# The second expert product of a mixture-of-experts block in three rounded parts from the 13th tile on

## The reference

```python
assign = jnp.argmax(x @ centroids.T, axis=1)          # one expert per row
for e in range(8):
    h = _layernorm(xs, ln_g[e], ln_b[e])
    h = jax.nn.relu(h @ w1[e].T + b1[e])              # 256 -> 1024 channels
    ye = xs + h @ w2[e].T + b2[e]                     # 1024 -> 256 channels
    y = y + jnp.where((es == e)[:, None], ye, 0.0)
out_sorted = alpha * y + (1.0 - alpha) * xs
```

## Time and profile before

| | us |
|---|---|
| median of three executions | 635.12 |
| the profiled execution | 630.98 |
| its span, first to last instruction | 629.2 |
| PE busy in the span | 587.4 (93%) |
| DVE busy | 342.7 (54%) |
| ACT busy | 292.6 (46%) |
| `up`, line 1183: PE busy | 147.5 |
| `down`, line 1199: PE busy | 141.8 |

### The profile page before, as it was taken

How to read it: one execution, slowest core, us unless ns; L and a number is a source line. 1 busy time by engine, 2 the same in 40 slices (tenths; PEclk the granted TensorE clock), 3 DMA queues, 4 the chain that set the end, 5 groups by cost and what they waited for, 6 DMA issues and landing times.

```text
span 629.2 us, 12344 instructions
## 1 busy us (share of the span) xinstructions
PE 587.4 (93%) x3638; PEld 499.5 (79%) x3639; DVE 342.7 (54%) x909; ACT 292.6 (46%) x727; POOL 254.5 (40%) x390
## 2 busy tenths in 40 slices
PE   3989999999999999997889998999999999999991
PEld 2557787787877778786789998998999999998980
DVE  1495987959697795988634353333222233322230
ACT  4565758677785867765542522222222222222320
POOL 7706163545646354554333353333333333333321
PEclk9998999999999999996989999999999999999996
DMA  8920111211211020111695575555555545555200
GB/s 311 408 71 1 34 35 34 101 35 69 67 66 37 1 102 1 68 34 67 218 347 166 185 228 208 185 185 193 183 205 217 196 179 182 190 215 190 94 5 0
DMA packets 25186, 83.59 MB, mean 133 GB/s; under 512 B 3821, under 2 KB 13423, under 8 KB 18992
## 3 DMA queue, kind: packets, MB, share of 16 engines
q1 hardware_dynamic: 16896, 59.57, 27.0%
q0 software_dynamic: 7552, 22.89, 10.0%
q10 hardware_dynamic: 688, 0.52, 0.3%
HBM read 70.35 MB, written 13.53 MB: 133 GB/s over the span
## 4 chain that ended last, share of the span: by engine, by line
PE 82%; DVE 6%; issue 3%; POOL 2%; DMA 2%; ACT 1%; DVEq 0%; POOLq 0%; ACTq 0%
PE bank_a L1183 20%; PE bank_l L1199 20%; PE bank_a L958 10%; PE bank_l L946 7%; PE bank_c L1062 4%; PE bank_a L987 4%; PE bank_b L1039 2%; PE bank_a L1003 2%; PE bank_a L996 2%; PE bank_b L1038 2%; DMA arena<-rows_by_expert,take_idx 2%; PE bank_c L1079 2%; PE bank_b L1024 2%; DVE arena L1274 2%; PE bank_b L1171 1%
## 5 line engine op out<-in xcount | busy, mean ns | idle before, releaser
L1183 PEld LDWEIGHTS bank_a<-masks,arena 128*128 128x128 f32 x1248 | 146.7, 194 | 1.8
L1183 PE MATMUL bank_a<-masks,arena 128*128 128x128 f32 x1248 | 147.5, 277 | 0.0
L1571 DVE TENSOR_TENSOR arena<-bank_a,b_col 128x512 f32<-128x512 f32 x78 | 54.0, 692 | 168.8 <-PE bank_a L1183 154.2
L1199 PE MATMUL bank_l<-w_sb,arena 128*128 x624 | 141.8, 380 | 3.0 <-issue 2.0
L1199 PEld LDWEIGHTS bank_l<-w_sb,arena 128*128 128x128 f32 x624 | 115.5, 190 | 18.7 <-issue 4.5
L663 POOL DMA_INDIRECT arena<-rows_by_expert,take_idx x39 | 41.3, 1058 | 156.3 <-DVE k_mix L1585 154.5
L1274 DVE TENSOR_TENSOR arena<-arena 128x256 f32<-128x256 f32 x224 | 93.8, 465 | 7.4 <-PE bank_l L946 7.3
L946 PEld LDWEIGHTS bank_l<-arena,k_mix 128*128 128x128 f32 x448 | 66.1, 198 | 39.6 <-ACT k_mix L712 26.8
L901 ACT ACTIVATE arena<-arena 128x512 f32<-128x512 f32 x78 | 44.9, 622 | 103.5 <-PE bank_l L1199 101.9
L958 PE MATMUL bank_a<-arena 128*128 128x512 f32 x160 | 81.9, 611 | 0.0
L891 ACT ACTIVATE masks<-bank_b,b_col,g_col 128x128 f32<-128x128 f32 x78 | 31.4, 453 | 107.6 <-PE bank_b L1171 107.6
(11 more groups left out here) (151 smaller groups left out, 780.5 us busy)
## 6 DMA issues: line engine op xcount, KB each, us to landing
arena<-w SPq DMA_DIRECT2D x39, 1024.0 KB, 4.8
arena<-x SPq DMA_DIRECT2D x16, 512.0 KB, 3.6
w_sb<-w SPq DMA_DIRECT2D x8, 1024.0 KB, 14.3
arena<-b SPq DMA_DIRECT2D x1, 1024.0 KB, 13.9
arena<-rows_by_expert,take_idx POOLq DMA_INDIRECT x39, 4.7
out<-k_mix,put_of POOLq DMA_INDIRECT x39, 3.7
rows_by_expert<-arena POOLq DMA_INDIRECT x32, 4.3
arena<-wk SPq DMA_DIRECT2D x1, 256.0 KB, 4.2
```

Source lines behind the costliest of these rows:

```text
L1183: m = pe.matmul(bank_a[k // 4][:, k % 4 * P:(k % 4 + 1) * P], w1_now[t.par][:, i * F + k * P:i * F + (k + 1) * P], xl_t[t.par % 2][:, i * ...
L1199: m = pe.matmul(bank_l[p][:, 0:D], h_act[:, k * P:(k + 1) * P], w2_sb[:, bass.ds(e * (FC * D) + k * D, D)], start=(k == 0), stop=(k == FC ...
L1571: dve.tensor_tensor(h_sb[:, n * 512:(n + 1) * 512].rearrange("p (k t) -> p k t", t=P), bank_a[n][:, :].rearrange("p (k t) -> p k t", t=P), ...
```

## The change

From tile 12 on (`in_parts(t)`) the second product is written as a sum of three. ACT no longer writes the relu to `h_act` but to `h_high`, a tensor of type float32r, a rounded float32. DVE forms the rest, `h_low` = relu(h) - `h_high` (`h_low_part`, one operation per half of 512 columns). In the same way, ACT copies the whole `w2` of the tile's expert, 128x2048, into `w2_high`, rounded (`high_part`), and DVE subtracts it from `w2` into `w2_low` (`w2_low_part`). There are two buffers of each, in turn. `down_in_parts` then has 24 matmuls of 256 columns on float32r operands where `down` has eight on float32: for each of the eight blocks `h_high` x `w2_high` and `h_high` x `w2_low`, and then for each of them `h_low` x `w2_high`. The product `h_low` x `w2_low` is left out.

The parts of `w2` for tile t+1 are made in turn t. On DVE the order of a turn changes too: `finish(t-1)`, two `h_low_part(t)`, two `bias_h(t+1)`, `w2_low_part(t+1)`. The addresses of the arena's buffers move; the sizes of the old ones do not.

```diff
+        h_low = lay3.take_rounded("h_low", F)
+        h_high = nc.alloc_sbuf_tensor_at("h_high", [P, F], F32R, offset=arena_at + 4 * h_at)[:, :]
+        w2_high = [lay4.take_rounded(f"w2_high{i}", FC * D) for i in range(2)]
+        w2_low = [lay4.take_rounded(f"w2_low{i}", FC * D) for i in range(2)]
...
+        def in_parts(t):
+            return not isinstance(t.half, int) or number(t) >= NA
...
-                    act.activation(h_act[:, w], h_sb[:, w], ACT.Relu).then_inc(s_hr, 1)
+                    act.activation((h_high if in_parts(t) else h_act)[:, w], h_sb[:, w], ACT.Relu).then_inc(s_hr, 1)
+            def high_part(t):
+                e = act.value_load(expert_of(t), min_val=0, max_val=E - 1)
...
+                need(act, s_ye, 1, before(t, 2), 1)
+                copy(w2_high[t.par % 2], w2_of(e)).then_inc(s_whi, 1)
             def turn(t):
                 relu(t)
+                if exists(before(t, -1)) and in_parts(before(t, -1)):
+                    high_part(before(t, -1))
                 if exists(before(t, -2)):
                     gains(before(t, -2))
...
+            def down_in_parts(t):
+                p = t.par % 2
+                need(pe, s_yb, 1, before(t, 2), 1)
+                need(pe, s_whi, 1, t, 1)
+                need(pe, s_wlo, 1, t, 1)
+                for k in range(FC):
+                    if k % 4 == 0:
+                        need(pe, s_hr, 2, t, k // 4 + 1)
+                    h, w = slice(k * P, (k + 1) * P), slice(k * D, (k + 1) * D)
+                    pe.matmul(bank_l[p][:, 0:D], h_high[:, h], w2_high[p][:, w], start=(k == 0), stop=False)
+                    pe.matmul(bank_l[p][:, 0:D], h_high[:, h], w2_low[p][:, w], start=False, stop=False)
+                for k in range(FC):
+                    if k % 4 == 0:
+                        need(pe, s_hlo, 2, t, k // 4 + 1)
+                    m = pe.matmul(bank_l[p][:, 0:D], h_low[:, k * P:(k + 1) * P], w2_high[p][:, k * D:(k + 1) * D],
+                                  start=False, stop=(k == FC - 1))
+                m.then_inc(s_ye, 1)
...
                 need(dve, s_hr, 2, t, 0)
+                if in_parts(t):
+                    need(dve, s_hlo, 2, before(t, 1), n + 1)
                 need(dve, s_h, 2, t, n + 1)
...
+            def w2_low_part(t):
+                e = dve.value_load(expert_of(t), min_val=0, max_val=E - 1)
+                need(dve, s_whi, 1, t, 1)
+                dve.tensor_tensor(w2_low[t.par % 2], w2_of(e), w2_high[t.par % 2], ALU.subtract).then_inc(s_wlo, 1)
+            def h_low_part(t, n):
+                need(dve, s_ye, 1, t, 0)
+                need(dve, s_hb, 2, t, n + 1)
+                need(dve, s_hr, 2, t, n + 1)
+                w = slice(n * 512, (n + 1) * 512)
+                dve.scalar_tensor_tensor(out=h_low[:, w], in0=h_sb[:, w], scalar=0.0, in1=h_high[:, w],
+                                         op0=ALU.max, op1=ALU.subtract).then_inc(s_hlo, 1)
             def turn(t):
...
+                if in_parts(t):
+                    finish(before(t, 1))
+                    for n in range(2):
+                        h_low_part(t, n)
+                    if one is not None:
+                        for n in range(2):
+                            bias_h(one, n)
+                        w2_low_part(one)
+                    return
```

More of the change, by code:

```diff
@@ L123, in build_program @@
         ARENA = 33808
-        arena_at = nc.sbuf_base
+        arena_at = -(-nc.sbuf_base // 32) * 32
         arena = sb("arena", [P, ARENA], F32)
+        assert nc.sbuf_base == arena_at + 4 * ARENA
         class Layout:
@@ L185, in build_program @@
         h_act = lay3.take(F)
+        h_at = lay3.at - F
+        lay3.at = dead_at - F
+        h_low = lay3.take_rounded("h_low", F)
+        h_high = nc.alloc_sbuf_tensor_at("h_high", [P, F], F32R, offset=arena_at + 4 * h_at)[:, :]
+        lay4 = Layout(dead_at, PHASE1_AB)
+        w2_high = [lay4.take_rounded(f"w2_high{i}", FC * D) for i in range(2)]
+        w2_low = [lay4.take_rounded(f"w2_low{i}", FC * D) for i in range(2)]
         earlier = lay2.take(P)
@@ L208, in build_program @@
         k_mix = [sb(f"k_mix{i}", [P, PAIRS * P], F32)[:, :] for i in range(2)]
-        b2_sb = lay3.take(E * D)
+        b2_sb = arena[:, h_at + F:h_at + F + E * D]
+        assert h_at + F + E * D <= dead_at - F
         ident = sb("ident", [P, P], F32)
@@ L334, in build_program @@
         s_hr = sem("h_ready")
+        s_whi = sem("w2_high_ready")
+        s_wlo = sem("w2_low_ready")
+        s_hlo = sem("h_low_ready")
         s_ye = sem("y_done")
@@ L462, in rounds, with w2_of @@
                 turn(Step(i // SLOTS, i % SLOTS, SLOTS))
+        def in_parts(t):
+            return not isinstance(t.half, int) or number(t) >= NA
+        def w2_of(e):
+            return w2_sb[:, bass.ds(e * (FC * D), FC * D)]
         def exists(t):
@@ L900, in relu @@
                     w = slice(i * F // 2, (i + 1) * F // 2)
-                    act.activation(h_act[:, w], h_sb[:, w], ACT.Relu).then_inc(s_hr, 1)
+                    act.activation((h_high if in_parts(t) else h_act)[:, w], h_sb[:, w], ACT.Relu).then_inc(s_hr, 1)
+            def high_part(t):
+                e = act.value_load(expert_of(t), min_val=0, max_val=E - 1)
+                if isinstance(t.half, int) and number(t) in (NA, NA + 1):
+                    need(act, s_o, 2, LAST_SEQ, 2)
+                    need(act, s_og, 2, LAST_SEQ, 2)
+                need(act, s_ye, 1, before(t, 2), 1)
+                copy(w2_high[t.par % 2], w2_of(e)).then_inc(s_whi, 1)
             def turn(t):
                 relu(t)
+                if exists(before(t, -1)) and in_parts(before(t, -1)):
+                    high_part(before(t, -1))
                 if exists(before(t, -2)):
@@ L911, in _ @@
             act.wait_ge(s_small, 64)
+            act.sem_inc(s_whi, 1 + NA)
             need(act, s_pick, 2 * MASKED, LAST_SEQ, 2 * MASKED)
@@ L1207, in turn @@
                     z_transposes(before(t, -2))
-                down(t)
+                if in_parts(t):
+                    down_in_parts(t)
+                else:
+                    down(t)
             pe.wait_ge(s_const, 1)
@@ L1595, in turn @@
                     bias_h(one, 1)
+                    if in_parts(one):
+                        w2_low_part(one)
             c = LAST_SEQ
+            dve.sem_inc(s_wlo, 1 + NA)
+            dve.sem_inc(s_hlo, 1 + 2 * NA)
             slots(LAST_BUT_ONE)
```

## The result

The changed kernel takes 616.51 us (median of four executions, 613.98 to 618.73) where the kernel before takes 635.15 (four, 634.54 to 640.68). The medians are 18.6 us apart. The ratio, as it was measured, is 0.9693, with a 95% interval of 0.9663 to 0.9724: 3.1% faster (the two medians alone give 2.9%). I had predicted 621 us with a range of 612 to 634, and a gain of 14.3 us. The profiled execution took 613.98 us, with a span of 612.2.

The account below looks back on a forecast made before the run. PE bound the old kernel; DVE was to bound the new: 20 x 6.9 + 6 x 6.6 + 3.1 = 180.7 us against 195.0, 14.3 less. Profiled 630.98 becomes 616.7, plus 4.14 for the median: 621 us, range 612 to 634.

Parts of the forecast that it names:

- the sum that led to 621: Stretch from tile 12 on, paced by DVE: 177.6 us plus 3.1 behind, 180.7 against 195.0.
- the first rival: Second products from tile 12: PE stays the bound, 27 products save 0.78 us each, 21.1 us, 614 us; chance 0.22.
- The price of the float32r matmul: New second product on PE: one pass per matmul, 24 x 0.112 = 2.68 us, making PE's turn 6.46 us.
- the third rival: New product on PE: weight load and pass don't overlap, turn 9.0 us, 681 us; chance 0.09 together with two passes.
- Two passes: New product on PE: float32r needs two passes, also 681 us; chance 0.09 together with load and pass apart.
- four passes: New product on PE: float32r runs like float32, 186 us more, 821 us; chance 0.02.
- The operations of DVE and ACT: New 2048-column operations per tile: DVE's subtraction for w2_low 2.29 us, ACT's rounded copy 1.87 us.
- DVE becomes the bound, narrowly: From tile 12 on, DVE's turns of 6.9 and 6.6 us exceed PE's 6.46; chance 0.55 for 617 to 626 us.
- the sum of the DVE turn: DVE's operations and blocks per tile, start to start: 6.9 us in the loop, 6.6 us behind it.
- The second rival: DVE's number-load blocks run behind operations, not beside them: 7.5 us per turn, 638 us; 7.1 to 7.5 us given 0.10.
- Cover: ACT's turn of some 4.5 us, copy included, is hidden; DVE's new order makes nothing late at first.

## Why the prediction was right, and where not

- **The time** of 616.51 us lies in the range of 612 to 634, but the sum that led to 621 had the wrong bound. The range holds the measured time because it took in the first rival too, so that hit is in part luck.
- **The price of the float32r matmul** was right in kind, one record per matmul, and 4% low in size: 2.79 us for 24 against 2.68. Sixteen are 114 ns apart, the last eight 120. The PE turn is 6.58 and not 6.46. The Trainium skill ("FP8 and Floating Point Precision", TensorE Precision Notes) lists, beside true FP32 with its four passes, a reduced precision that reads the 4-byte FP32 and truncates it. It gives no number of passes for this one. The trace has one record per matmul, every 114 to 120 ns, close to the 107 ns that the prediction works out for 256 columns passing once.
- **Load and pass apart**, the third rival, is refuted: one load record of 188 to 191 ns and one matmul of 256 columns fit into each interval of 114 to 120 ns. The Trainium skill's rule ("TensorE: Matmul & The Clock Gate", Part 3, The mechanism), that a load overlaps with matmuls in flight only when the row group differs, does not agree with this trace. Two passes and four passes are refuted by the same rows.
- **The operations of DVE and ACT** came out as worked out: 2293 ns for 2.29 us, 1895 ns for 1.87.
- **"DVE becomes the bound, narrowly" failed.** The first rival, PE stays the bound, is what happened; I gave it 0.22 and 614 us. The failed step is the sum of the DVE turn: 6.9 us in the loop, where it is 6.0 with nothing to wait for, and 6.6 behind it, where it is 5.6. I had read 0.83 to 1.05 us between the starts of two operations as what a block with a load of the expert's number costs beside one operation before it, and charged 0.93 three times. In the turn shown with the low part made twice, where DVE does not wait, the two `h_low` take 1.20 us from the first start to the first bias (513.02 to 514.22), where I had 0.72 + 0.93; the two biases take 1.68 up to `w2_low_part`, where I had 2 x 0.93; the second half of `finish` takes 0.40, where I had 0.57. What still shows is mostly the block ahead of `w2_low_part`, with 0.15 to 0.5 us, and not in every turn. The rows that I used were of a DVE that had just waited for a semaphore. In the new turn it is busy all along, and an operation of 2.29 us stands ahead of the blocks. That the sequencer works ahead by several blocks behind a long operation, and had nothing prepared after a wait, is my reading of these gaps; no run isolates it.
- **The size of the gain.** With PE as the bound the trace has 27 x 0.67 + 1.9 = 20.0 us, against my 14.3; the medians are 18.6 us apart. That the rival's 21.1 us comes close is luck in part: it had 3.0 us too much for the matmuls (27 x 0.11) and nothing for the 1.9 us of pauses. The prediction took PE's load of the expert's number as hidden and did not look at the two long turns of the kernel before.
- **The second rival**, the block behind the operation, is refuted by the same turn: 6.0 us, not 7.5.
- **Cover.** That ACT's copy and the order on DVE are hidden is shown by the run with the float32 product, at 0.9986.

## What to carry to other kernels

A float32 product with 256 moving columns per matmul can be paid for in three rounded products, 116 ns each in the mean, instead of two records of 216 ns, if the product of the two low parts may be left out and an engine with free time makes the parts; here the parts took 3.7 us of DVE and 1.9 of ACT per tile for 0.67 us of PE, and were free only because both engines had that time. With 128 columns it should lose, by an estimate from the rows here: three matmuls of 109 ns against the two records of 112 ns of an `up`. Do not charge an idle engine's start-to-start times to the same engine when it is full: sum its durations and small gaps, then double one of its operations and read its own turn. Before such a product is begun earlier, look at what the other queues must deliver sooner.

## What the runs showed of the hardware that was not expected

POOL's tiny operation on `put_of`, 128x1, takes 323 ns in the mean before, 1583 ns after, and 2529 ns with the low part made twice. Two of its rows in the changed kernel:

```profile
507.48 2.27 POOL L689 TENSOR_SCALAR put_of<-arena,skip 128x1 int32<-128x1 f32 x1
...
514.04 2.29 POOL L689 TENSOR_SCALAR put_of<-arena,skip 128x1 int32<-128x1 f32 x1
```

It starts 0.2 us after DVE's operation of 2048 columns (507.30 and 513.87 above) and ends 0.16 to 0.17 us after that has ended. Its time follows that of DVE's operation: the median is 1.26 us where DVE makes half the low part (1.23 us), 2.28 in the changed kernel (2.29 us), and 3.76 where DVE makes it twice. So a DVE operation with two SBUF inputs holds up a POOL operation that reads SBUF; the Trainium skill says this in "SBUF — State Buffer", section SBUF: two separate sides, where the shared port pair is an exclusive lock, also for a DVE operation with two SBUF inputs against a GpSimd operation that reads SBUF. POOL's instructions for the gathers grow too, from 1058 to 1223 ns in the mean, those for the scatters of the result from 1014 to 1063; no run shows why. In the changed kernel POOL has time for all of this; the start from tile 5 shows where it has not.
